# Expert-FFN kernel: gated result rows scattered by an adding DMA into two sums, merged by one adding transfer

## The reference

```python
# stage 1, per token of sequence b
h      = gelu(x @ fc1_w.T + fc1_b)                    # 128 -> 512
y      = concat(h @ fc2_w.T + fc2_b,                  # 96 shared columns
                h @ experts_w[idx[b]].T + experts_b[idx[b]])   # 32 columns of the sequence's expert
# stage 2, routed FFN over 8 experts, two of them for each token
scores = y @ router_w.T
top_v, top_i = top_k(scores, 2);  routing_w = softmax(top_v)
out = sum over e of  (gelu(y @ w1[e].T) @ w2[e].T) * w_e      # w_e: the token's weight of expert e
return x + out
```

## Time and profile before

| | |
|---|---|
| executions | 344.18, 346.32, 340.74 us |
| span of the profiled execution | 320.1 us |
| its own time around the span | not recorded apart; median less span 24.1 us |
| TensorE busy | 235.2 us (73%), mean granted clock 0.881 |
| VectorE / ScalarE / GpSimd busy | 188.4 / 178.5 / 185.9 us |
| scatters into `slots` (line 583) | 64, 68.0 us busy, 20.1 us of gaps |
| scatters into `results` (line 603) | 80, 86.9 us busy |
| last scatter begins | 289.29 us |
| DMA moved | 57.90 MB, mean 181 GB/s |

### The profile page before, as it was taken

The page is one execution under the profiler, slowest core; times in us unless marked ns, Lnnn a source line. Parts: engine busy times, 40 slices in busy tenths (PEclk is TensorE's granted clock), DMA queues, the critical chain, the costliest instruction groups (busy, mean ns, idle before and its releaser), DMA issues.

```text
span 320.1 us, 5181 instructions
## 1 busy us (share of the span) xinstructions
PE 235.2 (73%) x1138; PEld 180.7 (56%) x1138; DVE 188.4 (59%) x471; ACT 178.5 (56%) x265; POOL 185.9 (58%) x203
## 2 busy tenths in 40 slices
PE   7974999979877326799999999798977979700000
PEld 2653776657655201578888888697856868600000
DVE  2568988578576470077776775465454665501880
ACT  4888577578461230296767666476555555401830
POOL 3009587777777774005776777565736656662660
PEclk9999799979979957699999999899999979955555
DMA  4395234329611153557775776847856664214981
GB/s 133 101 333 177 73 96 141 104 75 273 200 43 59 51 187 132 208 181 240 244 253 200 248 288 240 314 173 250 265 194 250 199 234 156 98 33 133 361 248 46
DMA packets 32611, 57.90 MB, mean 181 GB/s; under 512 B 5544, under 2 KB 15920, under 8 KB 32594
## 3 DMA queue, kind: packets, MB, share of 16 engines
q1 hardware_dynamic: 23778, 43.76, 39.1%
q0 software_dynamic: 4608, 8.54, 8.3%
q10 hardware_dynamic: 4208, 5.42, 6.0%
HBM read 20.56 MB, written 13.02 MB: 105 GB/s over the span
## 4 chain that ended last, share of the span: by engine, by line
PE 23%; issue 22%; POOL 22%; DMA 18%; DVE 5%; ACT 4%; SPq 3%; POOLq 1%; DVEq 0%; ACTq 0%
POOL slots L583 15%; PE hp L359 11%; DMA results<-rows,back_now 10%; PE dn L372 8%; POOL results L603 4%; DMA slots<-y_rows,slot 4%; PE dx L1069 2%; POOL ffn L624 2%; PE tr L1084 1%; DMA ffn<-results 1%; ACT hs L397 1%; ACT hid L387 1%; SPq L450 1%; DMA ffn_raw<-in_w2T 1%; DVE ffn L983 1%
## 5 line engine op out<-in xcount | busy, mean ns | idle before, releaser
L603 POOL DMA_INDIRECT results<-rows,back_now x80 | 86.9, 1086 | 49.6 <-POOL back_now L595 20.7
L583 POOL DMA_INDIRECT slots<-y_rows,slot x64 | 68.0, 1063 | 22.2 <-issue 20.1
L359 PE MATMUL hp<-xs,w 128*128 128x512 f32 (+1 forms) x288 | 66.7, 367 | 11.3 <-DVE xs L950 11.3
L406 DVE TENSOR_TENSOR hs<-hid,hs 128x1024 fp32r<-128x1024 f32 (+1 forms) x64 | 69.7, 1089 | 8.9 <-ACT hs L397 7.7
L387 ACT ACTIVATE hid<-hp 128x1024 f32<-128x1024 f32 (+1 forms) x48 | 42.4, 883 | 51.4 <-PE hp L359 45.5
L372 PE MATMUL dn<-hs,w 128*128 128x512 f32 (+1 forms) x288 | 67.6, 371 | 0.0
L359 PEld LDWEIGHTS hp<-xs,w 128*128 128x128 f32 x288 | 49.4, 192 | 22.4 <-issue 9.9
L397 ACT ACTIVATE hs<-hid 128x1024 fp32r<-128x1024 f32 (+1 forms) x64 | 60.9, 952 | 1.1
L372 PEld LDWEIGHTS dn<-hs,w 128*128 128x128 f32 x288 | 48.7, 194 | 7.5
L959 DVE COPY rows<-tr 128x512 f32<-128x512 f32 (+1 forms) x24 | 14.4, 602 | 34.2 <-POOLq L568 32.6
L359 PE MATMUL hp<-xs,fc 128*128 128x512 f32 x96 | 28.3, 436 | 0.0
(11 more groups left out here) (123 smaller groups left out, 246.6 us busy)
## 6 DMA issues: line engine op xcount, KB each, us to landing
w<-ffn SPq DMA_DIRECT2D x48, 512.0 KB, 3.7
ffn<-results SPq DMA_DIRECT2D x16, 256.0 KB, 5.5
picked<-slots ACTq DMA_DIRECT2D x14, 264.0 KB, 3.5
x_raw<-in_xT SPq DMA_DIRECT2D x8, 256.0 KB, 3.2
cexp_raw<-in_cexpT SPq DMA_DIRECT2D x32, 64.0 KB
out<-ffn SPq DMA_DIRECT2D x8, 256.0 KB, 3.9
results<-rows,back_now POOLq DMA_INDIRECT x80
picked<-slots ACTq DMA_DIRECT2D x8, 132.0 KB
```

What stands on the lines that cost most here:

```text
L359: mm = pe.matmul(dst, weight[:, w, cols], xs[:, st.parity, v, 0:width], start=m == 0, stop=m == len(passes) - 1)
L406: dve.tensor_tensor(by_block(k, st, hs[:, st.parity, 1, g, :]), by_block(k, st, hid[:, g, :]), by_block(k, st, hs[:, st.parity, 0, g, :].b ...
L583: pool.indirect_dma_start(out=slots, out_offset=bass.IndirectOffsetOnAxis(ap=slot[:, u, n:n + 1], axis=0), in_=y_rows[:, u, k, r, :], in_o ...
L603: pool.indirect_dma_start(out=results, out_offset=bass.IndirectOffsetOnAxis(ap=back_now[:, u, r:r + 1], axis=0), in_=rows[:, u, r, :], in_ ...
```

## The change

`results`, its bounds check and the whole last part are gone. Instead there are two sums in DRAM, the output itself and `odd_sums`, each with 512 rows more than there are tokens, for the filler rows. SyncE copies `x` into the output, DRAM to DRAM, and writes zeros over `odd_sums` and the 512 extra rows of both, where it loaded `x_rows` before. Even tiles scatter into the output and odd tiles into `odd_sums`, with an adding DMA. Filler rows carry the numbers of the extra rows and a gate of zero, and are sent too. At the end one adding DMA of GpSimd adds `odd_sums` to the output.

The gate is computed per chunk in stage 1 as 0.5 ± 0.5·tanh(gap / 2): a `Tanh` on ScalarE and two small VectorE instructions, which write it into the column behind the destination number. In stage 2 VectorE scales each block of 128 rows by its gate as it moves them out of `tr`: 4 instructions for a wide tile, 2 for a narrow one.

```diff
-    results = nc.dram_tensor("results", (TOPK * TOKENS, P), F32, kind="Internal").ap()
+    odd_sums = nc.dram_tensor("odd_sums", (TOKENS + DUMP, P), F32, kind="Internal").ap()
+    sums = (out, odd_sums)
+    def whole(t):
+        return t[0:TOKENS, :].rearrange("(a b) d -> a (b d)", b=SUM_COLS // P)     # 256 rows of 2048 floats
...  SyncE, behind the loads of stage 1
-            sp.wait_ge(s_pool_lo, POOL_EXP)
-            sp.dma_start(x_rows[:, :, :], x_all).then_inc(s_xrows, 16)
+            sp.dma_start(whole(out), x.rearrange("s (q b) d -> (s q) (b d)", b=SUM_COLS // P)).then_inc(s_sums, 16)
+            sp.wait_ge(s_zeros, 1)
+            sp.dma_start(odd_sums[0:TOKENS, :].rearrange("(p n r) d -> p n (r d)", p=P, r=RPT),
+                         zeros[:, :].unsqueeze(1).to_broadcast((P, TOKENS // DUMP, RPT * P))).then_inc(s_sums, 16)
+            for t in sums:
+                sp.dma_start(t[TOKENS:TOKENS + DUMP, :].rearrange("(p r) d -> p (r d)", r=RPT), zeros[:, :])\
+                  .then_inc(s_sums, 16)
...  SyncE, the end: the loads of results and the stores are gone
-                sp.dma_start(z_rows[:, g, k, :], result_groups[:, k, g, :])
-                sp.dma_start(out_store[:, g * FIN_GROUP:(g + 1) * FIN_GROUP, :], ...)
+            sp.wait_ge(s_out, 16)
...  GpSimd, constants and fillers
-            pool.memset(filler[:, :, P:P + 1].bitcast(I32), NO_ROW).then_inc(s_filler, 1)
+            pool.iota(filler[:, :, P:P + 1].bitcast(I32), [[1, RPT], [0, 1]], base=TOKENS, channel_multiplier=RPT)
+            pool.memset(zeros[:, :], 0.0).then_inc(s_zeros, 1)
...  GpSimd, send_back
                     pool.indirect_dma_start(
-                        out=results, out_offset=bass.IndirectOffsetOnAxis(ap=back_now[:, u, r:r + 1], axis=0),
-                        in_=rows[:, u, r, :], in_offset=None,
-                        bounds_check=TOPK * TOKENS - 1, oob_is_err=False).then_inc(s_zout[u], 16)
+                        out=sums[u], out_offset=bass.IndirectOffsetOnAxis(ap=back_now[:, u, r:r + 1], axis=0),
+                        in_=rows[:, u, r, :], in_offset=None, compute_op=ALU.add).then_inc(s_zout[u], 16)
+            pool.wait_ge(s_sums, 16 * 4)           # ahead of the first send_back
...  GpSimd, the end: add_second is gone
+            for u in range(2):
+                pool.wait_ge(s_zout[u], 16 * Step(TILES // 2 - 1, u).blocks_upto())
+            pool.dma_start(whole(out), whole(odd_sums), accum_op=ALU.add, max_dma_last_dim=4 * SUM_COLS).then_inc(s_out, 16)
...  ScalarE, step_a, between the high part of half 0 and the work on half 1; the Exp and the Gelu behind it are gone
+                if (st - 2).within(CHUNKS):
+                    wait(act, s_gap, (st - 2).value + 1)
+                    act.activation(lean[:, :], gap[:, :], ACT.Tanh, scale=0.5).then_inc(s_lean, 1)
...  VectorE, place_pairs; the copy of the numbers at 847 becomes two
+                wait(dve, s_lean, st.value + 1)
+                for k in range(TOPK):
+                    dve.tensor_scalar(y_rows[:, st.parity, k, :, P + 1:P + 2].rearrange("p r w -> p (r w)"), lean[:, :],
+                                      k - 0.5, 0.5, ALU.mult, ALU.add)
...  VectorE, step_c
-                    dve.tensor_copy(rows[:, done.parity, 0:blocks, :], tr[:, 0:blocks, :]).then_inc(C.rows, 1)
+                    for r in range(blocks):
+                        ins = dve.tensor_scalar(rows[:, done.parity, r, :], tr[:, r, :],
+                                                back[:, bass.ds(done.value, 1), r, 1:2].rearrange("p t w -> p (t w)").bitcast(F32),
+                                                None, ALU.mult)
+                    ins.then_inc(C.rows, 1)
```

More of the change, by code:

```diff
@@ L243, in build @@
         slot = sb("slot", [P, 2, RPT * TOPK], I32)
[L244 to L247, removed]
+        gap = sb("gap", [P, RPT])
+        lean = sb("lean", [P, RPT])
         count = sb("count", [P, EXP])
@@ L270, in build @@
         end_i = sb("end_i", [P, EXP], I32)
-        back = sb("back", [P, TILES, RPT], I32)
+        back = sb("back", [P, TILES, RPT, 2], I32)
         back_now = sb("back_now", [P, 2, RPT], I32)
@@ L312, in build @@
         s_zout = [sem(f"s_zout{n}") for n in range(2)]
-        s_z = [sem(f"s_z{n}") for n in range(GROUPS)]
-        s_gate = sem("s_gate")
-        s_half, s_second, s_fin = sem("s_half"), sem("s_second"), sem("s_fin")
+        s_zeros = sem("s_zeros")
         s_out = sem("s_out")
@@ L554, in _ @@
             pool.wait_ge(s_filler, 1)
-            pool.memset(filler[:, :, P:P + 1].bitcast(I32), NO_ROW).then_inc(s_filler, 1)
+            pool.iota(filler[:, :, P:P + 1].bitcast(I32), [[1, RPT], [0, 1]], base=TOKENS, channel_multiplier=RPT)\
+                .then_inc(s_filler, 1)
             with pool.Fori(0, POOL_EXP) as e:
@@ L731, in _ @@
             run_tiles(act, step_c)
[L734 to L738, removed]
-                for r in range(FIN_GROUP):
-                    ins = act.activation(z1[:, r, :], z1[:, r, :], ACT.Copy,
-                                         scale=gate[:, 1, g * FIN_GROUP + r:g * FIN_GROUP + r + 1])
-                ins.then_inc(s_second, 1)
-            for g in range(GROUPS):
-                scale_second(g)
         @block_ctx.vector
@@ L846, in step_a @@
                     wait(dve, s_yfree, done.value + 1)
[L847 to L849 removed]
+                    for k in range(TOPK):
+                        dve.tensor_copy(y_rows[:, done.parity, k, :, P:P + 1].bitcast(I32).rearrange("p r w -> p (r w)"),
+                                        out_row[:, bass.ds(done.value, 1), :].rearrange("p c r -> p (c r)"))
                     dve.tensor_copy(y_rows[:, done.parity, 0, 0:RPT - 1, 0:P], three[:, :, 0:P])
@@ L935, in _ @@
             dve.tensor_scalar(owner_i[:, :], owner_f[:, :], float(EXP - 1), None, ALU.min).then_inc(s_where, 1)
-            dve.wait_ge(s_exp, 1)
-            link(dve.tensor_scalar(denom[:, :], egap[:, :], 1.0, None, ALU.add))
-            link(dve.reciprocal(gate[:, 0, :], denom[:, :]))
-            dve.tensor_tensor(gate[:, 1, :], egap[:, :], gate[:, 0, :], ALU.mult).then_inc(s_gate, 1)
             def split_picked(st):
@@ L973, in _ @@
             run_tiles(dve, step_c)
-            dve.wait_ge(s_xrows, 16)
-            def finish(g):
-                dve.wait_ge(s_z[g], 16 * TOPK)
-                z0 = z_rows[:, g, 0, :].rearrange("p (s d) -> p s d", d=P)
-                for r in range(FIN_GROUP):
-                    s = g * FIN_GROUP + r
-                    ins = dve.scalar_tensor_tensor(z0[:, r, :], z0[:, r, :], gate[:, 0, s:s + 1], x_rows[:, s, :],
-                                                   ALU.mult, ALU.add)
-                ins.then_inc(s_half, 1)
-            for g in range(GROUPS):
-                finish(g)
         @block_ctx.tensor
```

65 lines of the change are left out of this document (16 added, 49 removed).

## The result

The changed kernel is **slower**: 368.94 us (363.25 to 372.8) against 342.46 us (340.38 to 346.32) beside it, a ratio of 1.067, interval 1.057 to 1.078. A second comparison gave 1.084 (1.069 to 1.100). Ratios and intervals are taken over a kernel's fast executions alone, those within 1.5% of its fastest, while a time without a ratio is the median over all its executions. The prediction was 346.9 us, no difference beyond 2%. The time lies in its range of 331 to 386 us, but the mechanism is that of the second rival, the work of an adding scatter on GpSimd.

A forecast was written before the change was run, and what follows sets the result against it. No single engine bound it: GpSimd paced stage 1, TensorE the wide tiles, waits on buffers and landings the pairs. Terms -8.1 + 2.0 + 0.5 + 4.8 + 3.5 = +2.7 us, added to the median: 346.9 us, range 331 to 386.

The forecast's parts named there:

- the second rival: Making descriptors for adding scatters on GpSimd grows: 362 us at +0.3 us a scatter, 415 at +0.96; chance 0.27.
- The adding scatter on GpSimd: Return scatters in stage 2: +0.1 us each, nothing in wide tiles, +4.8 us over the eight pairs.
- The threshold: Wide tiles of stage 2: from +0.12 us a scatter on, GpSimd sets their pace as well.
- The rival's working: Descriptor cost in stage 2: 8 tile intervals beyond 0.49 us of room, plus 8 pairs of six scatters each.
- the reading of 4.7 us from a scatter to its landing: Stage 2 pairs: a scatter starting at 0 has landed at about 4.7 us; anything added comes back once a pair.
- My argument against that rival: GpSimd scatters of 528 and 512 bytes, with and without bounds check, all take 0.96 to 0.98 us.
- The landing: Adding scatters in stage 2 land +0.5 us later, once in each of seven pairs: +3.5 us; wide tiles 0.
- Rows out of PSUM: VectorE in stage 2: one copy becomes four of 0.28 us, +0.5 us over the kernel, up to 3.
- The end: Behind the last scatter: 28.7 us replaced by one adding transfer of 20.6 in all, gain 8.1 us, bounds 15.1 and 1.1.
- Stage 1: Gates per chunk 0.8 us and filling the sums 1.2 us, together +2.0 us.
- Tables: ScalarE in stage 1: if Tanh shares no table with Gelu, two loads a chunk, +9 us, 356 us; chance 0.10.
- What lies around the span: Median 24.1 us above the 320.1 us span, left as it is; the forecast difference is added to the median.

The follow-up runs named there:

- e9: Changed kernel with plain scatters, each behind a GpSimd memset of 128x800 floats: 347.72 us, ratio 1.077 to the kernel before.
- e6: Changed kernel with a tile's four scatters cut to 32, 64, 96 and 128 rows, adding in even tiles, plain in odd ones: 362.21 us.
- e11: Changed kernel whose last transfer copies the second sum over the first and does not add: 344.52 us.
- e10: Changed kernel with plain scatters, rows taken out of PSUM by one copy and gates left out: 311.93 us, ratio 0.966 to the kernel before.
- e8: Changed kernel with the bounds check back in the adding scatter, so filler rows are not sent: 367.8 us, ratio 1.065.
- e3: Changed kernel with a plain scatter in place of the adding one, all else the same: 331.69 us.
- e7: Changed kernel without adding scatter, fill or x: plain scatters skip fillers, output of twice the tokens, adding merge kept: 339.17 us beside 344.82 for before.
- e1: Kernel before, no edit, run again for a second profile: 338.26 us.
- e12: Kernel before with gates carried with the rows, applied by one broadcast multiplication, x added from SBUF at the end: 332.67 us, ratio 0.992.

## Why the forecast missed and its range held, point by point

- **The adding scatter on GpSimd** is the step that failed. I took +0.1 us, "near the plain scatter, the row of the same shape". It measured +0.58 (1.55 against 0.97). The threshold was right: the room was 0.12 us a scatter, and beyond it wide tiles went from 6.46 to 8.14. The rival's working at +0.58 is 8 x (2.32 - 0.49) = 14.6 us for the wide tiles and 8 x 3.48 = 27.8 for the pairs, 42 in all. Measured are 15.3 and 15.9 in the wide tiles, which agrees, and 19.2 and 23.3 in the pairs. The working left out that GpSimd's longer work takes the place of waits for landings: these fell from 11.4 us to 3.9 and 7.2 (e9), and 27.8 less the difference is 20.3 and 23.6. The same waits show that the reading of 4.7 us from a scatter to its landing was too simple: in the chain, the scatter at 217.28 has landed after 3.80, and 0.9 more is GpSimd's way to the next scatter.
- My argument against that rival, that the duration "does not look bound to details of a row", was true and beside the point: e6 shows that most of the price comes with the kind of instruction, and little of it with the rows. *DMA: Bandwidth & Descriptors* of the Trainium skill calls descriptor generation small and variable. The trace agrees that rows cost little (0.1 us from 32 to 128 plain rows), and not that an instruction does.
- **The landing**, +0.5 us: measured 0 to 0.6, 0.6 by the last scatter alone and 0 to 0.4 over all (e11 against e10, less the 0.58). I summed it to 3.5 us. The waits leave some 1 to 5 us for it (e9). That the filler rows hold up the landings is out by e8.
- **Rows out of PSUM**, +0.5 us and "up to 3": measured 4 to 7, between kernels with plain scatters (e3 and e7 against before, e1, e10 and e12). That they lie in the loop from a freed buffer to the next scatter is an argument; and what they cost beside adding scatters, where GpSimd sets the pace, no run shows. I had costed a block at 0.28 us by a copy; it took 0.345.
- **The end**, -8.1: measured -10.1 by span. From the last landing on it took 18.0 us where I had 20.6. The merge took 13.5 us with its descriptors and landing, where I had 14.0 + 1.0 + 2.3 = 17.3; the closing behind it took 3.9 where I had 3. So the transfer was sized too large and the closing too small. That both reads count fits the copy's 8.3 us and is not settled by it (e11).
- **Stage 1**, +2.0: measured 0.3 to 2.8 where it had no stalls (e11, e9 and e10 against before).
- **Tables**: no load but the first one. ScalarE, by line:

```profile
L663 ACT ACTIVATE lean<-gap 128x4 f32<-128x4 f32 x8 | 1.6, 194 | 1.4 <-DVE gap L778 1.4
L613 ACT ACT_TABLE_LOAD x1 | 1.3, 1283 | 0.7 <-PEq L1084 0.7
```

  `Tanh` ran between the `Gelu`s without a load, where `Exp` had cost two. *ScalarE: Activation LUTs* of the Trainium skill (section on table sets) lists tanh beside exp and gelu apart; the trace does not agree that this means a load.
- **What lies around the span**: I read the 24.1 us between span and median as surroundings. The changed kernel's profiled execution took 363.25 us for a span of 361.5, so the surroundings are 1.75. The rest were most likely stalls of stage 1 that the first profile did not have, as e1's span of 337.9 with them says. As I added a difference to the median, it did not spoil the sum.
- **The range** held by luck. Its top of 386 came from +0.6 us a scatter, a figure that no row gave; the scatter measured +0.58.

## What to carry to other kernels

Before a change makes an instruction dearer on an engine that issues in order, compute that engine's own pace beside the stage's: here it had 0.12 us a scatter to spare, and the unknown price was 0.58. Measure such a price alone first, at two sizes, for a price per instruction is not saved by sending less. In this kernel a gate per row came free on VectorE as one broadcast multiplication in place of the copy out of PSUM (601 against 602 ns), and cost some 4 to 7 us of stage 2 as four small ones.

## What the runs showed of the hardware

- A scatter that adds costs GpSimd 1.55 us against 0.97 for 128 rows of 512 bytes, and 1.38 against 0.89 for 32 rows: mostly a price per instruction.
- Adding rows go out one by one. The GpSimd queue had 13840 packets for 4608: with the 64 stage 1 scatters at 32 packets each and 272 for the merge (4880 - 144 x 32 in e3), an adding scatter of 128 rows has 144 packets, and a plain one 32. e6 bears this out. Its total is

```profile
q0 software_dynamic: 7952, 9.45, 14.3%
```

  which is what comes out if an adding scatter of n rows has n + 16 packets and a plain one 32 at any of the four lengths.
- Adding 2.1 MB from DRAM to DRAM took 13.5 us in 272 packets, copying it 8.3 in 48.
- `Tanh` and `Gelu` needed no table load between them.
- 128x512 out of PSUM with a broadcast factor takes VectorE 0.60 us, four blocks of 128x128 with a factor per partition 4 x 0.345.
- Stage 1 of one and the same program ended at 124.8 and at 140.9 us in two executions. In the longer one VectorE waited up to 5.9 us at a time on something outside the trace, and GpSimd behind it 3 to 8 us.
